# Attention stage: products with the values moved to the two side banks, a third bank for the maxima, side work in blocks, and two stores of the q and k parts

## The reference, cut to what matters

```python
q, k, v = (qkv[0], qkv[1], qkv[2])                     # from x @ w_qkv
scores = jnp.einsum('bhqd,bhkd->bhqk', q, k) * SCALE
scores = jnp.where(causal[None, None], scores, -jnp.inf)
geo_bias = q_proj[..., :, None] * k_proj[..., None, :]  # rank-one bias of each head
scores = scores + head_scales[None, :, None, None] * geo_bias
attn = jax.nn.softmax(scores, axis=-1)
```

## Time and profile before

| | us |
|---|---|
| median of 3 runs | 2678.53 (2677.25 to 2684.58) |
| the profiled execution | 2683.27, its span 2681.3 |
| TensorE busy | 2320.9 (87% of the span) |
| VectorE, ScalarE, GpSimd busy | 1624.2, 1314.3, 435.1 |
| mean granted TensorE clock | 0.925 of full speed |

### The profile page before, as it was taken

One profiled execution on the slowest core, in us unless ns is written; L12 is line 12 of the kernel. 1 busy time (PEld: TensorE's weight loads), 2 busy tenths in 40 slices (PEclk: granted clock), 3 DMA queues, 4 the chain that ended last, 5 costly groups with the idle time before them and its releaser, 6 DMA issues. The chain is left out here.

```text
span 2681.3 us, 45165 instructions
## 1 busy us (share of the span) xinstructions
PE 2320.9 (87%) x15010; PEld 1680.5 (63%) x15010; DVE 1624.2 (61%) x3570; ACT 1314.3 (49%) x2260; POOL 435.1 (16%) x364
## 2 busy tenths in 40 slices
PE   7999999998799996588888888888888875169997
PEld 6666667666688884455555555555555565158996
DVE  4666767675444546656666666665666555766664
ACT  3565656564445554555555554555555543034442
POOL 0000000000111114210000000000000022046664
PEclk8999999999899997799989998999999987579998
DMA  4300000000000001232222222332222128145542
GB/s 113 110 0 0 0 0 0 0 0 17 15 0 0 0 0 39 50 81 76 77 71 74 72 73 70 73 76 71 72 72 72 38 92 280 47 130 123 127 93 32
DMA packets 122975, 156.64 MB, mean 58 GB/s; under 512 B 26896, under 2 KB 104096, under 8 KB 122784
## 3 DMA queue, kind: packets, MB, share of 16 engines
q1 hardware_dynamic: 104480, 129.85, 17.7%
q0 software_dynamic: 14336, 25.44, 4.9%
q10 hardware_dynamic: 4096, 0.53, 0.1%
HBM read 96.26 MB, written 58.98 MB: 58 GB/s over the span
## 5 line engine op out<-in xcount | busy, mean ns | idle before, releaser
L1386 DVE TENSOR_REDUCE at_top<-psum 128x1 f32<-128x512 f32 (+3 forms) x1024 | 456.7, 484 | 346.9 <-PE psum L1122 346.6
L1567 ACT ACTIVATE out_x<-psum 128x512 f32<-128x512 f32 (+1 forms) x768 | 385.4, 536 | 449.5 <-PE psum L1140 448.1
L1120 PE MATMUL psum<-out_x 96*128 96x512 bf16 (+3 forms) x1024 | 292.9, 312 | 59.5 <-DVE at_top L1386 42.3
L1138 PE MATMUL psum<-out_x 98*128 98x512 bf16 (+3 forms) x1024 | 289.0, 309 | 60.9 <-DMA out_x<-at_neg_top 37.8
L1122 PE MATMUL psum<-at_mask_q,at_ident_b 128*128 128x128 bf16 x1024 | 205.0, 226 | 0.0
L1120 PEld LDWEIGHTS psum<-out_x 96*128 96x128 bf16 x1024 | 102.6, 100 | 162.4 <-DVE at_top L1386 105.1
L1140 PE MATMUL psum<-at_mask_k,at_ident_b 128*128 128x128 bf16 x1024 | 202.5, 224 | 0.0
L1138 PEld LDWEIGHTS psum<-out_x 98*128 98x128 bf16 x1024 | 101.5, 99 | 159.3 <-issue 70.8
L1156 PE MATMUL psum<-out_x,at_values 128*32 128x512 f32 (+3 forms) x2048 | 165.7, 467 | 0.8 <-ACT out_x L1567 0.8
L2360 POOL DMA_INDIRECT out<-ex_result,slot_tokens x64 | 119.5, 1868 | 102.9 <-DVE ex_result L2492 88.3
L1156 PEld LDWEIGHTS psum<-out_x,at_values 128*32 128x32 f32 x2048 | 64.1, 116 | 94.3 <-issue 79.0
(11 more groups left out here) (400 smaller groups left out, 5896.1 us busy)
## 6 DMA issues: line engine op xcount, KB each, us to landing
out_x<-qk_parts SPq DMA_DIRECT2D x128, 192.0 KB
out_x<-qk_parts SPq DMA_DIRECT2D x128, 128.0 KB
qk_parts<-at_q_parts SPq DMA_DIRECT2D x96, 128.0 KB
qk_parts<-at_k_parts SPq DMA_DIRECT2D x96, 128.0 KB
x_residual<-in_x SPq DMA_DIRECT2D x16, 512.0 KB, 3.9
out_x<-qk_parts SPq DMA_DIRECT2D x128, 64.0 KB
token_rows<-ro_h_tok SPq DMA_DIRECT2D x16, 512.0 KB, 3.0
token_rows<-ro_gate_row SPq DMA_DIRECT2D x16, 512.0 KB, 4.1
```

The source lines that it names most:

```text
L1120: pe.matmul(out, q_stack[0:STACK, h, qt * P:(qt + 1) * P], k_stack[0:STACK, h, 0:w], start=True, stop=True)
L1138: pe.matmul(bank(bk)[:, col:col + w], k_stack[0:STACK + N_SHIFT, h, kt * P:(kt + 1) * P], q_stack[0:STACK + N_SHIFT, h, kt * P:T], start=T ...
L1386: dve.tensor_reduce(top[:, h, qt:qt + 1], bank(MAX0 + n % 2)[:, col:col + w], AX.X, ALU.max).then_inc(mxr.sem, 1)
L1567: act.activation(probs[:, slot(h), 512 * f:512 * f + w], bank(f)[:, 0:w], ACT.Exp).then_inc(ex.sem, 1)
```

## The change

- The products with the values go to bank 5 and bank 7 in turn (`PV_BANK` is now a table by group). Bank 6 becomes a third bank for the maxima (`MAX_BANK`), one bank for each fill, so that a fill waits for the same fill of the head before. The turned maxima go to bank 6 too; so fill 2 of the maxima waits for the negation in heads 1, 5, 9 and 13, and `dve_neg_max` now stands between VectorE's reductions of fills 0 and 1.
- As the side banks are shared, TensorE gets other waits before the products with the values (the values kept, the hT copies read, the output normalised) and before some side work (`oe`, the copy to `oT`). The turn of the second half of the result moves from head 12 to head 11.
- VectorE and ScalarE do their side work in blocks after all three fills of a head, some of it a head earlier than before.
- The two DMAs of the maxima rows move from ScalarE's queue to SyncE (`sp_row`). SyncE's order for a batch becomes: row 1, q store, k store, row 2, loads 0 and 1 of the next batch, row 3, load 2, row 0 of the next batch, load 3. The very first row stays on ScalarE.
- The partition order of q and k becomes (feature, head) by permuted weight columns in setup, so that a side is stored by one DMA (`N_STORES` 2 in place of 12).

```diff
-            n = 3 * h + f
-            if n >= 2:
-                pe.wait_ge(*mxr(b, 4 * ((n - 2) // 3) + (1, 3, 4)[(n - 2) % 3]))
+            if h:
+                pe.wait_ge(*mxr(b, 4 * (h - 1) + MAX_DONE[f]))
...
+        MAX_BANK, MAX_DONE = (MAX0, MAX0 + 1, MAX2), (1, 3, 4)
+        PV_BANK = (SIDE_A, SIDE_B, SIDE_A, SIDE_B)
...
                     if f == 2 and h % GROUP == 0 and not (first and h == 0):
-                        pe.wait_ge(*neg(i, N_SHIFT * (h // GROUP + 1)))
+                        if h == 0:
+                            pe.wait_ge(*(xs(i - 2, 2) if last else hTf(i + 1, DK)))
+                        elif h == GROUP:
+                            pe.wait_ge(*(on(i - 1, 3) if last else ve(i + 1, 2)))
+                        else:
+                            pe.wait_ge(*on(i, h // GROUP - 1))
                         pe_pv(pe, *((i, h // GROUP - 1) if h else (i - 1, NG - 1)))
                     pe_scores(pe, i, h, f, first)
+                    if f == 1 and turn_max:
+                        pe_turn_max(pe, *after)
+                    if f == 2 and turn_max:
+                        pe.wait_ge(*neg(after[0], N_SHIFT * (after[1] + 1)))
                     if h + AHEAD < HEADS:
                         pe_max(pe, i, h + AHEAD, f)
...
+                    if f == 1 and h % GROUP == 1 and not (last and h + GROUP > HEADS):
+                        g = h // GROUP
+                        dve_neg_max(dve, *((i, g + 1) if g + 1 < NG else (i + 1, 0)))
...
+                if h in (0, 1) and not last:
+                    for n in range(2):
+                        act_qk(act, i + 1, 2 * h + n)
+                    for n in range(2):
+                        act_qk2(act, i + 1, 2 * h + n)
+                if h == 3 and not last:
+                    act_values(act, i + 1)
+                if h == 14 and turn:
+                    for k in range(DK):
+                        act_hT(act, i + 2, k)
+                    for k in range(DK):
+                        act_hT_hi(act, i + 2, k)
...
-            for j in range(3):
-                for m in range(2):
-                    sp.dma_start(parts_dram[side, j, :, 8 * m:8 * m + 8, :].rearrange("c h t -> h c t"),
-                                 qk_parts[side][:, j, m, :]).then_inc(stored.sem, 16)
+            sp.dma_start(parts_dram[side].rearrange("j m c h t -> (c h) (j m) t"),
+                         qk_parts[side][:, :, :, :].rearrange("p j m t -> p (j m) t")).then_inc(stored.sem, 16)
...
+        def sp_row(sp, b, g):
+            sp.wait_ge(*neg(b, N_SHIFT * (g + 1)))
+            for j in range(N_SHIFT):
+                sp.dma_start(q_stack[STACK + j:STACK + j + 1, GROUP * g:GROUP * (g + 1), :].rearrange(
+                    "a h (q p) -> a (h q) p", p=P), neg_top[:, j, :]).then_inc(row[g].sem, 16)
+
+        def sp_batch(sp, i, last):
+            sp_row(sp, i, 1)
+            if not last:
+                sp_store(sp, i + 1, 0)
+                sp_store(sp, i + 1, 1)
+            sp_row(sp, i, 2)
+            if not last:
+                sp_load(sp, i + 1, 0)
+                sp_load(sp, i + 1, 1)
+            sp_row(sp, i, 3)
+            if not last:
+                sp_load(sp, i + 1, 2)
+                sp_row(sp, i + 1, 0)
+                sp_load(sp, i + 1, 3)
```

More of the change, by code:

```diff
@@ L1277, in pe_batch @@
                         pe_turn_delta(pe, i - 1, 0)
-                if h == 12 and not first:
+                if h == 11 and not first:
                     pe.wait_ge(*xs(i - 1, 1))
@@ L1466, in dve_batch @@
[L1466 to L1475, removed]
@@ L1486, in dve_batch @@
-                    if h == 15 and f in (0, 2) and norm:
-                        dve_hT_lo(dve, i + 2, (f // 2,))
+                if h in (0, 1) and not last:
+                    for n in range(2):
+                        dve_qk_rest(dve, i + 1, 2 * h + n)
+                if h == 4 and not first:
+                    dve_normal(dve, i - 1, 3, SIDE_B)
+                if h == 6 and not first:
+                    dve_o_lo(dve, i - 1)
+                if h == 7:
+                    dve_normal(dve, i, 0, SIDE_B)
@@ new lines, in dve_batch @@
+                if h == 10:
+                    dve_normal(dve, i, 1, SIDE_A)
+                    if not first:
+                        dve_add(dve, i - 1, 0)
+                if h == 11 and not first:
+                    dve_add(dve, i - 1, 1)
+                if h == 8 and norm:
+                    dve_stats(dve, i + 2)
+                    dve_moments(dve, i + 2)
+                if h == 12 and norm:
+                    dve_norm(dve, i + 2)
+                if h == 13:
+                    dve_normal(dve, i, 2, SIDE_A)
@@ L1656, in act_batch @@
[L1656 to L1673, removed]
-                            act_hT(act, i + 2, 1)
-                        if (h, f) == (15, 1):
-                            act_hT_hi(act, i + 2, 1)
+                if h % GROUP == 0 and not (first and h == 0):
+                    act_keep_oT(act, *((i, h // GROUP - 1) if h else (i - 1, NG - 1)))
@@ new lines, in act_batch @@
+                if h in (0, 1) and not last:
+                    for n in range(2):
+                        act_qk(act, i + 1, 2 * h + n)
+                    for n in range(2):
+                        act_qk2(act, i + 1, 2 * h + n)
+                if h == 3 and not last:
+                    act_values(act, i + 1)
+                if h == 6 and not first:
+                    act_o_hi(act, i - 1)
+                if h in (8, 9) and not first:
+                    act_delta(act, i - 1, h - 8)
@@ L1788, in sp_load @@
                     sp.wait_ge(turned, HALF_X)
-            elif g == 1:
-                sp.wait_ge(*(loaded[0](0, loaded[0].per) if isinstance(b, int) and b == 0 else row[2](b - 1, row[2].per)))
+            elif g == 1 and isinstance(b, int) and b == 0:
+                sp.wait_ge(*loaded[0](0, loaded[0].per))
             for side, n, parts in LOADS:
-                src = parts_dram[side, parts, :, GROUP * g:GROUP * (g + 1), :]
+                h0 = GROUP * g % M_HEADS
+                src = parts_dram[side, parts, g // 2, :, h0:h0 + GROUP, :]
                 if src.shape[0] == 1 and n[1] - n[0] > 1:
```

107 lines of the change are left out of this document (41 added, 66 removed).

## The result

The changed kernel takes 2703.3 us (median of 4, 2702.3 to 2706.1), the kernel before 2678.3 in the same session: ratio 1.009, interval 1.0073 to 1.0108. It is 25 us slower. The forecast was 2589, with a range that ended at 2650, so it was wrong in sign.

The account below looks back on a forecast made before the run. TensorE, waiting 8 us per batch, was nearest its bound. Cycle 58.6 + 0.7 + 0.4 = 59.7 against 65.77; 14 x 6.1 = 85, + 5 + 1 - 1 = 90 gained: 2593, as median 2589 us; range 2560 to 2650.

Parts of the forecast that it names:

- The compute steps: Attention cycle from zero (head 0's third score product) to head 8: stretches of 15.9, 9.15 and 2.65 us.
- the whole walk: One attention cycle followed in the new order with today's durations: 58.6 us against 64.87.
- The waits that were put on the negation: TensorE's third maximum product waits for VectorE in heads 1, 5, 9 and 13: 1.2, 0.5, 0.85, 1.65 us.
- The main term: Head 7: the row of group 2, issued by SyncE ahead of load 0, lands in time; 3.9 us gained.
- The queue: SyncE's loads and maxima rows: landings about meet the needs of heads 9 and 12; cost 0.7 us, between 0 and 4.2.
- The rule that I cited: A SyncE DMA uses only as many lowest-numbered engines as divide its outermost dimension; used for the loads' two-engine tail.
- Batch 0 and 15: First and last attention batches: 5 us gained (0 to 7) and 1 (-1 to 3); setup costs 1.
- Slower: SyncE's order: One queue for rows, stores and loads: a 25 us pair makes group 3's row 7 late; about 2706 us, 9%.
- The wait moves: Row of group 3 or load 0 comes late each batch: cycle 63.2 us, about 2639 in all; 23%.
- sparse spots: Stretches of the cycle where TensorE's clock might fall: 0 to 1.6 us, taken as 0.4.
- that rival: The clock falls more, once a batch in sparse stretches such as heads 13 and 15: cycle 61.3, 2612 us; 6%.
- The two stores: Two stores instead of twelve: no cost as long as a store takes under 11 us, and no gain.

Follow-up runs that it names:

- kernel 5: kernel 1 with the q copies in DMAs of 16 rows each, 9 DMAs per load instead of 6; 2573.5 us, ratio 0.9599.
- kernel 1: The changed kernel with parts and features adjacent again in the DRAM copy, two stores per side; 2623.2 us, ratio to before 0.978.
- kernel 8: The changed kernel, its layout and two stores kept, with every load cut into DMAs of 16 rows, 12 per load instead of 6; 2572.5 us, ratio 0.9591.
- kernel 2: The kernel before with only the changed kernel's DRAM layout of the parts; 2679.5 us, ratio 0.9987.

## Why the prediction was wrong

- *The compute steps*, zero to head 8: right within 0.2 us in each stretch, in the changed kernel itself. Where the loads are out of the way (kernel 5) the whole walk holds: predicted 58.6 us per cycle, measured 58.72. The waits that were put on the negation (1.2, 0.5, 0.85, 1.65), 4.2 us a cycle, are shown as 3.3 (45.7 us over 14); the stretches agree all the same, so the rest of that time lies where the profile shows no wait. A cut of kernel 5's timeline at the predicted places:

```profile
1533.22 0.28 PE L1143 MATMUL psum<-out_x 98*128 98x256 bf16 x1
...
1549.32 0.39 PE L1143 MATMUL psum<-out_x 98*128 98x512 bf16 x1
...
1558.57 0.38 PE L1143 MATMUL psum<-out_x 98*128 98x512 bf16 x1
...
1561.34 0.38 PE L1143 MATMUL psum<-out_x 98*128 98x512 bf16 x1
...
1571.06 0.39 PE L1143 MATMUL psum<-out_x 98*128 98x512 bf16 x1
...
1579.51 0.38 PE L1143 MATMUL psum<-out_x 98*128 98x512 bf16 x1
...
1592.20 0.28 PE L1143 MATMUL psum<-out_x 98*128 98x256 bf16 x1
```

  that is 16.10, 9.25, 2.77, 9.72, 8.45 and 12.69, against 15.9, 9.15, 2.65, 9.8, 8.4 and 12.7.
- *The main term* (head 7 shorter by 3.9 us): right, 3.8.
- *The queue*: this step failed: "So a load is about 8.1 us of those two engines, plus 2 from issue to first traffic", and from it "lands at 33.3", 9.8 us after an issue at 23.5. (The two terms make 10.1, so 33.6, and a margin of 0.2 and not 0.5 even as it stands.) Load 0 was issued at 24.0 and landed at 37.8; head 9 began at 33.98 and asked for it at 34.4. Two things were wrong, and kernel 1 parts them. First, the load was taken as half of the pair. With the shape of the loads as before, and the pair as long as predicted, load 0 still lands 12.2 to 13.2 us after its issue, about 3 more than the 9.8: by then more than half of load 1, issued right behind it, had moved too. Second, the length was read from the kernel before and carried over as if the loads did not change. With the half between part and feature the k loads went from all engines to 3 and 2, a lone load from 8.5 to 11.5 us, the pair from 17.3 (kernel 1) to about 23.7 us (1555.25 to 1579), and load 0's landing to 13.8 to 15.9: about 2 more.
- *The size of the miss.* I took 0.7 us for this term and bounded it by 4.2. The cycle shown takes 65.58 us, 7.0 over the walk: 5.2 in heads 8 and 9 (the wait of 3.40, and most of the rest the slow clock behind it), 1.0 in heads 10 to 12 (0.66 the row of group 3), 0.7 in the other four stretches together. The mean of the 14 is 66.22.
- *The rule that I cited* bears on the change itself. The Trainium skill (DMA: Bandwidth & Descriptors, "Why a DMA increments its semaphore by 16 and not by 1") makes the number of engines depend on the outermost dimension. I applied it to the tail of today's loads and not to the changed line `parts_dram[side, parts, g // 2, ...]`. Kernels 1 and 8 agree with the rule: merging the dimension, or cutting to 16 rows, shortens a lone load from 11.5 us to 8.5 and about 6.
- *Batch 0 and 15*: 5 and 1 us of gain and 1 of cost in setup were taken. Measured, batch 0 ends 9.9 us later, and what follows the cycles takes 4.5 more. Setup and batch 0 wait 23.0 us for loads, against 8.8. With the q copies cut too (kernel 5) batch 0 ends at 1179.56, 9.8 us earlier than before, and the rest is 3.3 us shorter.
- *The rivals*: "Slower: SyncE's order" named a longer pair of loads as what would turn the sign, from 23.5 us on, and 2706 us. The pair took 23.7 and the time was 2703. Its place was wrong in part (load 0 in head 9 first, the row of group 3 only 0.66), and its reason (stores and rows in between) too. It had 9%. So that the number fits to 3 us is in part luck. "The wait moves" is the milder form of the same. The granted clock in the cycles of kernel 5 was 1.00, so the sparse spots left by the blocks do not lower it there. The rule of the Trainium skill that was cited with that rival (TensorE: Matmul & The Clock Gate, "A second HAM failure mode: psum-queue depth-cycling"), that short idles between groups of matmuls can switch the clock to and fro, was not borne out by this kernel.
- *The two stores*: right that they cost nothing: each lands in about 3.5 us, against the 11 allowed. Nor is a gain seen: kernel 8 with two stores takes 2572.5, kernel 5 with four 2573.5.

## What to carry to other kernels

A change of a DRAM layout is a change of every DMA that reads it. Look at which dimensions still merge, and what the outermost one becomes; a broadcast of 2 or 3 copies or an outer dimension of 3 left most DMA engines idle here, and the DMA share in short windows showed it (0.19 is three of sixteen). When the compute order is tightened, each transfer is asked for earlier: put its landing, not its issue, beside the new time of need, and count a margin near zero as a wait. When a second transfer is issued right behind it, the first does not land after half of the pair (here 12.2 us of 17.3).

## What the runs showed of the hardware that was not expected

- At a share of 0.19 (3 of 16 engines) the loads moved 78 GB/s, 26 per engine; at 0.13 (2 of 16) 54. The same rows, cut for all engines, moved 157 GB/s over a whole load (kernel 5), so the number of engines, not the memory, was the limit. The single 768 KB store with 128 rows outermost landed in 3.5 us.
- In kernel 2 longer loads gave shorter cycles (64.96 against 65.77): about three waits of 1.2 us in place of one of 2.3, and a granted clock of 0.96 against 0.94. That the shorter waits are what spared the clock was not tested by itself.
- In kernel 5 waits of up to 1.4 us in every cycle left the granted clock at 1.00 over 822 us. In the cycle shown of the changed kernel it fell to 0.50 during the wait of 3.40.
